# Attention scores in squares of 64 by 64 columns, and row deviations spread by a transpose

## What is computed

```python
# before the layers
mean = jnp.mean(x, axis=-1, keepdims=True)
var = jnp.mean(jnp.square(x - mean), axis=-1, keepdims=True)
normed = (x - mean) * jax.lax.rsqrt(var + LN_EPS)
# in each layer, 16 heads of 64, windows of 32 queries, n = 128
mask = (it < jb) | (it > jb + w) | (jb == -1)
sim = jnp.einsum('bhwie,bhwje->bhwij', bq, bk2) * QK_SCALE
sim = jnp.where(mask, -jnp.finfo(sim.dtype).max, sim)
attn = jax.nn.softmax(sim, -1)
out = jnp.einsum('bhwij,bhwje->bhwie', attn, bv2)
# feed-forward
xn = (x - mu) / jnp.sqrt(var + 1e-05) * g + bln
hg = xn @ W1 + b1
a, gate = jnp.split(hg, 2, -1)
return a * jax.nn.gelu(gate, approximate=False) @ W2 + b2
```

## Time and profile before

| What | Value |
| --- | --- |
| median of three runs | 5840.7 us |
| lowest and highest run | 5830.07 and 5843.88 us |
| profiled execution, its own time | 5848.61 us |
| span of that execution, first to last instruction | 5846.8 us |
| granted TensorE clock, mean | 0.937 |
| TensorE matmul records | 43296 |
| VectorE busy | 3854.6 us |
| ScalarE busy | 3254.7 us |
| GpSimd busy | 3175.1 us |

### The profile page before, as it was taken

How to read it: one execution, slowest core, us unless ns; L and a number is a source line. 1 busy time by engine, 2 the same in 40 slices (tenths; PEclk the granted TensorE clock), 3 DMA queues, 4 the chain that set the end, 5 groups by cost and what they waited for, 6 DMA issues and landing times. The chain is left out here.

```text
span 5846.8 us, 128835 instructions
## 1 busy us (share of the span) xinstructions
PE 5079.1 (87%) x43296; PEld 3299.7 (56%) x43296; DVE 3854.6 (66%) x6824; ACT 3254.7 (56%) x9898; POOL 3175.1 (54%) x1509
## 2 busy tenths in 40 slices
PE   4995899447589999999999999999999899987864
PEld 1331677334357765776577657765777477744542
DVE  2112000554289967997799769986999599956888
ACT  0000000332178866887588858884888488844432
POOL 0000000112389957996699759984999399930018
PEclk9999999759699999999999999999999999998975
DMA  7676555011100000000000000000000000000000
GB/s 208 166 181 143 117 108 109 24 59 50 38 7 0 0 16 5 0 0 16 5 0 0 16 5 0 0 0 20 1 0 0 20 1 0 0 16 14 7 2 14
DMA packets 271956, 199.78 MB, mean 34 GB/s; under 512 B 179032, under 2 KB 254264, under 8 KB 265336
## 3 DMA queue, kind: packets, MB, share of 16 engines
q1 hardware_dynamic: 202073, 119.60, 8.9%
q10 hardware_dynamic: 67487, 71.25, 4.2%
q0 software_dynamic: 2048, 4.20, 0.2%
HBM read 131.83 MB, written 63.16 MB: 33 GB/s over the span
## 5 line engine op out<-in xcount | busy, mean ns | idle before, releaser
L1800 POOL TENSOR_TENSOR rs<-ss,minus_half 128x16 f32<-128x16 f32 x386 | 1127.7, 2921 | 170.9 <-DVE ss L1877 168.8
L1718 ACT ACTIVATE s_ps<-s_ps,low 128x128 f32<-128x128 f32 x3072 | 1064.0, 352 | 1.1 <-DVE low L1888 1.1
L1798 POOL TENSOR_TENSOR t<-t 128x1024 f32<-128x1024 f32 x386 | 911.5, 2361 | 149.4 <-DVE t L1866 149.4
L1805 POOL TENSOR_TENSOR qk<-t,rs 128x1024 f32<-128x1024 f32 x386 | 734.3, 1902 | 60.5 <-POOL rs L1800 23.7
L1718 ACT ACTIVATION_READ_ACCUMULATOR s_ps<-s_ps,low 128x1 f32 x3072 | 673.3, 219 | 0.0
L1888 DVE TENSOR_REDUCE low<-s_ps 128x4 f32<-128x512 f32 x768 | 494.4, 685 | 150.0 <-PE s_ps L1546 150.0
L1897 DVE TENSOR_TENSOR p<-s_ps,rec 128x512 f32<-128x512 f32 x768 | 530.7, 691 | 30.5
L1860 DVE TENSOR_TENSOR t<-qk_ps,rot 128x1024 f32<-128x1024 f32 x386 | 472.4, 1224 | 95.1 <-PE qk_ps L1512 89.5
L1695 ACT ACTIVATE sq<-qk_ps 128x1024 f32<-128x1024 f32 x386 | 395.3, 1024 | 249.1 <-DVE t L1866 249.1
L1732 ACT ACTIVATE pT<-pT_ps 128x512 f32<-128x512 f32 x768 | 457.2, 595 | 104.2 <-PE pT_ps L1552 68.5
L264 PE MATMUL h_ps<-h_x,h_w 9*128 9x512 bf16 x4096 | 441.5, 628 | 84.3 <-DMA h_w<-rows_w1s 63.6
(11 more groups left out here) (404 smaller groups left out, 8781.6 us busy)
## 6 DMA issues: line engine op xcount, KB each, us to landing
h_x<-rows_xs SPq DMA_DIRECT2D x512, 72.0 KB
rows_hs<-h_parts ACTq DMA_DIRECT2D x88, 384.0 KB, 7.1
z_fm<-rows_hs SPq DMA_DIRECT2D x128, 144.0 KB
x_fm<-rows_hs SPq DMA_DIRECT2D x128, 144.0 KB
wqkv<-in_wqkv SPq DMA_DIRECT2D x7, 1536.0 KB, 6.6
o_w<-rows_exs ACTq DMA_DIRECT2D x512, 18.0 KB
rows_xs<-z_fm ACTq DMA_DIRECT2D x12, 384.0 KB, 5.5
rows_exs<-s_exp ACTq DMA_DIRECT2D x9, 512.0 KB, 6.7
```

What stands on the lines that cost most here:

```text
L1718: ins = act.activation(s_ps[:, e, i * P:(i + 1) * P], s_ps[:, e, i * P:(i + 1) * P], ACT.Exp, bias=low[:, c % 2, e, i:i + 1], scale=-1.0, ...
L1798: pool.tensor_tensor(t1[:, i, :], t1[:, i, :], t2[:, i, :], ALU.add).then_inc(s_["t12"], 1)
L1800: pool.tensor_tensor(rs[:, i, :], ss[:, i, :], R.minus_half[:, 0:2 * UH], ALU.pow).then_inc(s_["rs"], 1)
L1805: pool.tensor_tensor(qk[:, i, :].rearrange("p (h d) -> p h d", d=DH), t1[:, i, :].rearrange("p (h d) -> p h d", d=DH), rs[:, i, :].unsquee ...
```

## The change

It does two things. The scores of a pair of heads become four matmuls of 64 rows by 64 columns of the array rather than two of 64 by 128: for each e, queries 0 to 63 with keys 0 to 63, and queries 64 to 127 with keys 32 to 127. What is not computed keeps what the mask put there. And `spread` turns the column of `rstd` itself: four float32 transposes per group, each with one column of `rstd` repeated 128 times as what is turned. `diag`, its buffer, its semaphore and GpSimd's multiplication go; GpSimd's power now waits for the `spread` before it.

```diff
...
@@ -1320,10 +1319,11 @@
                     mm.then_inc(s_["var"], 1)
 
                 def spread(k):
-                    pe.wait_ge(s_["diag"], at(k))
+                    pe.wait_ge(s_["rstd"], at(k))
                     pe.wait_ge(s_["xn"], at(k - 1))
-                    pe.matmul(r_ps[:, :], R.ones[:, :], diag[:, :, :].rearrange("p b s -> p (b s)"),
-                              start=True, stop=True).then_inc(s_["spread"], 1)
+                    for b in range(GB):
+                        mm = pe.transpose(r_ps[:, col(b)], rstd[:, b:b + 1].to_broadcast([P, P]), R.ident[:, :])
+                    mm.then_inc(s_["spread"], 1)
 
                 def turn(n):
                     pe.wait_ge(s_["wTc"], at(n - 2))
...
@@ -1543,8 +1537,9 @@
                     for i in range(4):
                         for e in range(2):
                             r = slice(DH * e, DH * e + DH)
-                            mm = pe.matmul(s_ps[:, e, i * P:(i + 1) * P], qT[r, c % 2, i, :], kT[r, c % 2, i, :],
-                                           start=False, stop=True, skip_group_check=True)
+                            for q, k0, k1 in ((slice(0, 64), 0, 64), (slice(64, P), 32, P)):
+                                mm = pe.matmul(s_ps[q, e, i * P + k0:i * P + k1], qT[r, c % 2, i, q],
+                                               kT[r, c % 2, i, k0:k1], start=False, stop=True, skip_group_check=True)
                     mm.then_inc(s_["scores"], 1)
 
                 def turn_p(k, c, e):
...
@@ -1606,14 +1601,16 @@
 
                 def spread(l, j):
                     k = l * NG + j
-                    pe.wait_ge(s_["f_diag"], at(k))
+                    pe.wait_ge(s_["f_rstd"], at(k))
                     pe.wait_ge(s_["f_xn"], at(k - 1))
                     if j == 0:
                         pe.wait_ge(s_["kTc"], at(l * NU + NU - 1))
                     if j == 1:
                         pe.wait_ge(s_["p1"], at(l * NU + NU - 1))
-                    pe.matmul(r_ps[j], R.ones[:, :], diag[:, :, :].rearrange("p b s -> p (b s)"),
-                              start=True, stop=True).then_inc(s_["f_spread"], 1)
+                    for b in range(GB):
+                        mm = pe.transpose(r_ps[j][:, b * P:(b + 1) * P], rstd[:, b:b + 1].to_broadcast([P, P]),
+                                          R.ident[:, :])
+                    mm.then_inc(s_["f_spread"], 1)
 
                 def feed(l, j, t):
                     k = l * NG + j
...
@@ -1809,13 +1806,8 @@
 
                 def rstd_(k, j, c):
                     pool.wait_ge(s_["f_vare"], at(k))
-                    pool.wait_ge(s_["f_diag"], at(k - 1))
+                    pool.wait_ge(s_["f_spread"], at(k - 1))
                     pool.tensor_tensor(rstd[:, :], var[:, :], R.minus_half[:, 0:GB], ALU.pow).then_inc(s_["f_rstd"], 1)
-                    pool.wait_ge(s_["f_rstd"], at(k))
-                    pool.wait_ge(s_["f_spread"], at(k - 1))
-                    pool.tensor_tensor(diag[:, :, :], R.ident[:, :].unsqueeze(1).to_broadcast([P, GB, P]),
-                                       rstd[:, :].unsqueeze(2).to_broadcast([P, GB, P]), ALU.mult
-                                       ).then_inc(s_["f_diag"], 1)
 
                 norms(0, 0, 0)
                 norms(1, 1, 1)
```

More of the change, by code:

```diff
@@ L1261, in level2_cond @@
         rstd = m.sb("ad_rstd", [P, GB])
-        diag = m.sb("ad_diag", [P, GB, P])
         xn = m.sb("ad_xn", [P, GT])
@@ L1269, in level2_cond @@
         w_ps = [m.ps(f"ad_w_ps{i}", [P, 1024], BF16) for i in range(2)]
-        names = ("hid", "relu", "adapt", "sum", "center", "sq", "var", "var_eps", "rstd", "diag",
+        names = ("hid", "relu", "adapt", "sum", "center", "sq", "var", "var_eps", "rstd",
                  "spread", "xn", "z", "wT", "wTc")
@@ L1366, in rstd_ @@
                     pool.wait_ge(s_["var_eps"], at(k))
-                    pool.wait_ge(s_["diag"], at(k - 1))
+                    pool.wait_ge(s_["spread"], at(k - 1))
                     pool.tensor_tensor(rstd[:, :], var[:, :], R.minus_half[:, 0:GB], ALU.pow).then_inc(s_["rstd"], 1)
-                    pool.wait_ge(s_["rstd"], at(k))
-                    pool.wait_ge(s_["spread"], at(k - 1))
-                    pool.tensor_tensor(diag[:, :, :], R.ident[:, :].unsqueeze(1).to_broadcast([P, GB, P]),
-                                       rstd[:, :].unsqueeze(2).to_broadcast([P, GB, P]), ALU.mult
-                                       ).then_inc(s_["diag"], 1)
                 slots([(rstd_, 2)])
@@ L1458, in level2_layers @@
         rstd = m.sb("ff_rstd", [P, GB])
-        diag = m.sb("ff_diag", [P, GB, P])
         xn = m.sb("ff_xn", [P, GT])
@@ L1473, in level2_layers @@
                  "pTc0", "pTc1", "o", "oTc", "proj", "res",
-                 "f_xs", "f_center", "f_xc", "f_sq", "f_var", "f_vare", "f_rstd", "f_diag", "f_spread", "f_xn",
+                 "f_xs", "f_center", "f_xc", "f_sq", "f_var", "f_vare", "f_rstd", "f_spread", "f_xn",
                  "f_xa", "f_z", "f_gel", "f_h", "f_down", "f_res")
```

## The result

| | before | after |
|---|---|---|
| median of 4 runs each | 5838.0 us | 5775.4 us (5767.4 to 5791.8) |
| after / before, 95% interval | | 0.990 (0.987 to 0.992) |
| profiled execution, span | 5846.8 us | 5765.6 us |
| granted clock | 0.937 | 0.939 |

The change saves 1.0% of the time (0.8 to 1.3), 60 us of 5838. The forecast was 5780 us and a saving of 61.

The account below looks back on a forecast made before the run. TensorE was taken as the bound, alone in feed-forward and closely followed in attention, where VectorE holds the longer units. Terms -35 - 20 - 6 = -61 took 5848.6 to 5788, less 7.9 for the median: 5780 us, range 5755 to 5805.

Parts of the forecast that it names:

- The scores: Attention units: the step from mask to transposes falls from 1.21 to 1.12 us, times 384 units, -35 us.
- Four squares at once: Score step: a group of four records costs its longest, 0.082 us, so eight groups take 0.66.
- The change of division: Between mask and scores on TensorE: dividing the array differently adds 0.10 us.
- The hidden load of 0.05: Before the first score: a first weight load that nothing hides adds 0.05 us.
- it should pass through in full: Attention units, TensorE-paced (7.61 us) or VectorE-held (7.77 us): both contain the scores whole, so any change of that step reaches the unit.
- The spreads in the layers: Feed-forward stages: four transposes (0.43 us) replace two records (0.86), 8 times in 6 layers, -20 us.
- The adapter: Level 2's adapter: its deviations' spreads get shorter, two of them at the low clock, -6 us.
- GpSimd's work at nothing: Feed-forward stages: removing GpSimd's 48 multiplications of 1.04 us gains nothing, as GpSimd idles there.
- The power's new wait at nothing: Feed-forward groups: GpSimd's power, delayed some 3 us by waiting for the preceding spread, costs nothing.
- Pairs of records: Rival, score step: only two records run at a time, step 1.56 us, +108 in all, 5949 us; chance 0.12.
- The floor on the rate: Rival, score step: each record takes at least 0.028 us, step 1.34 us, +24 in all, 5865 us; chance 0.18.
- A unit that doesn't shrink: Rival, attention: scores shorten but another chain (ScalarE or GpSimd) holds the unit; 5815 us; chance 0.11.

Follow-up runs that it names:

- experiment 4: Changed kernel with the mask also written in 64 by 64 squares, a semaphore increment between waits and mask: 5773.9 us, 0.9907 of before.
- 9: Changed kernel with the 96-key score product cut into two tiles of 64 by 32, 48 score records a unit: 7552.9 us, 1.293 of before.
- 3: Changed kernel with each score square moving all 128 keys, still 32 records: 5874.6 us, 1.0091 of before.
- 7: Changed kernel with the mask in squares and the three waits moved ahead of the last value record, no increment: 5849.5 us, 1.0018 of before.
- 10: Changed kernel with GpSimd's removed multiplication put back as dead work: 5786.5 us, 0.9922 of before.
- 1: Kernel before the change with the new scores alone, spreads as before: 5812.3 us, 0.9972 of before.
- 2: Changed kernel with the old scores, so the new spreads alone: 5811.6 us, 0.9962 of before.
- 6: Changed kernel with all scores in tiles of 64 rows by 32 columns, 64 records a unit: 5899.2 us, 1.0105 of before.
- 11: Changed kernel with the 96-key product cut in two as in 9, records sorted with all 64-column tiles first: 5998.1 us, 1.0304 of before.
- the later kernels: Changed kernel with 10's dead work, and changed kernel with 64 by 32 score tiles in two units of eight: 0.9922 and 0.9917 of before.

## Why the prediction was right

**The scores, -35 us forecast, -24 measured: right in every part, a little undersized in cost.** Four squares at once, at the price of the longest: 0.083 us where 0.082 was said. The change of division: 0.10 as said, and taken away by experiment 4. By the Trainium skill, TensorEngine Tiling (Array Packing), section Key Properties, changing the tiling mode drains TensorE; the runs agree, at about 0.1 us each time (0.10 in 4; in 9 0.148 from start to start where a repeat takes 0.06), and a change from 64 to 32 columns with the same rows counts as one. The hidden load of 0.05 is there too, but behind the first record (0.133 in place of 0.083), not ahead of it. Step 1.14 us in place of 1.12, mostly that the four squares end apart from each other; of the 0.07 saved, 0.063 reached the unit. That "it should pass through in full" holds for both kinds of unit. The reading behind it was too kind to TensorE: that in the shorter kind no step of it waits is right by some 0.005 us only, and VectorE's product releases the mask in 240 of 372 units, not in 66 of 768 records. The gain passes even so, since the product itself waits for the scores.

**The spreads in the layers, -20 us forecast, about -20 from the eight groups and up to -29 with what lies around them.** 0.86 became 0.44. Between the first and last `feed` record the gain is 2.95 us a stage, what seven spreads come to. The rest of the stretch varies by more than 1 us from kernel to kernel with no edit there (last mask to first `feed`: 18.3 to 21.0 us on average over all kernels but 9), so nothing more is credited to the change.

**The adapter, -6 us forecast, -17 in that execution.** The clock rose to the upper level earlier there: the windows over its steps have 0.70 before and 0.89 after. Twelve profiled kernels with the new spreads have it at 44.2 to 67.5 us, median 57.8, two with the old ones at 61.2 and 65.7. The changed kernel's own profile has the lowest of all, so its -17 is mostly the clock's. Kernels in which the clock rose at the same group can be compared: 61.2 us before (clock 0.70) against 56.1 to 56.2 in 3, 7, 9 and 10 (0.68), and 65.7 in 1 (0.63) against 59.3 in 2, 4, 6 and 11 (0.64). That is 5.0 and 6.4 us for the new spreads, as forecast, with one old kernel in each comparison.

**GpSimd's work at nothing: not contradicted** (10). **The power's new wait at nothing: right**, 297 us of waiting [after, line 1810] and no group longer.

**The rivals.** Pairs of records: refuted by the spacing. The floor on the rate, 0.028 us a record: refuted, 32 records go at 0.021 in the changed kernel and 64 at 0.010 in experiment 6 (0.65 and 0.63 us from the first start to the last). The prediction's 0.028 counts up to the next step's start; so counted, the changed kernel has 0.026. From first to last start level 3 of the kernel before has 0.025 (32 records from 5317.05 on, 28 of them in the earlier trace rows), so it was nearer to 0.021 than it looked. Its limit of 0.024 for a loss is that of the scores alone; with the 26 us of the spreads the whole change would turn to a loss from 0.026. The Trainium skill, TensorE: Matmul & The Clock Gate, section Wait — 56ns, not 53.3ns?, has about 25 ns as the least start to start; that doesn't hold across squares that work side by side here. Within one tile the closest repeats were 0.058 us in the changed kernel (64 keys) and about 0.03 in experiment 6 (32 keys), so there nothing went below it. A unit that doesn't shrink: refuted, it followed within 0.007.

That the total fell within 5 us of the forecast is partly luck: the scores saved 11 us less than said, and the later kernels put the whole nearer 47 (0.8%) than 60. Added up from the traces, 24 + 20 + 5 or 6, it comes to about 50.

## What to carry to other kernels

Cut a product into squares of the array to leave out columns that a mask kills, not to run more records: squares go side by side at the price of the longest, and lose if all columns are moved. Count the changes of tile shape in the order of the records, sort by shape, and reckon with 0.1 us for each that is left; where shapes alternated from product to product, each change cost 0.19. Before moving a wait ahead of other work, set the end of what it waits for beside the start of that work: a constant distance (here 0.146 us) in every unit tells that it is the one that holds, even where the view of waits is silent. Before unrolling or splitting adds instructions to a loop, look at the instruction packets: a loop body that is refetched costs microseconds each pass, and shows as an idle time whose reason is "issue" at its head.

## What the runs showed of the hardware

- Squares of one shape are issued side by side and keep their own time: those that moved 64 keys ran ahead at 0.058 us while those that moved 96 went at 0.083.
- In eight tiles of 64 rows by 32 columns, 64 fp32 records started within 0.63 us, 0.010 each; the densest step of 32 in the trace of before has 0.025.
- A change of the tile's columns with the same rows took 0.148 us from start to start one way, 0.146 the other, where a repeat takes 0.058. With 48 records unsorted the step took 3.90 us, sorted 1.19.
- With 704 matmul records in a pass of TensorE's loop there was no stall at its head; with 768 there was one in 18 or in 36 of the 36 further passes, with 896 in all 36, each with nine or ten more instruction packets. A stalled unit was 2.5 to 7 us longer in 6 and 11.
- TensorE's next record started 0.144 to 0.147 us after the end of the product of VectorE that it waited for, and 0.256 with a semaphore increment between wait and record, which cost 0.11 us a unit.
